# Where the query projection stands in a step of an fp32-exact attention kernel

## The reference

```
q, k, v = x Wq^T, x Wk^T, x Wv^T          # 32 query heads, 8 key/value heads, 128 wide
q, k = rope(rmsnorm(q)), rope(rmsnorm(k))
keys, values = cache (512 rows, by block table) + the 128 new ones
probs = softmax(q keys^T * scale, cached keys beyond the length masked)
x = x + (probs values) Wo^T
h = x W^T + 2 * sum over the top 2 of 8 experts of gate * (x A_e^T) B_e^T
x = x + h
```

## Time and profile before

| | |
|---|---|
| time, median of 3 runs | 1186.98 us (1186.64 to 1187.24) |
| the profiled execution | 1185.75 us |
| its span, first to last instruction | 1183.9 us |
| granted TensorE clock, mean of the span | 0.994 |
| TensorE matmul busy | 1147.6 us, 97% |
| TensorE weight loads (beside the matmuls) | 1023.2 us, 86% |
| ScalarE busy | 934.6 us, 79% |
| VectorE busy | 923.4 us, 78% |
| GpSimd busy | 766.8 us, 65% |
| DMA | 98.11 MB, 83 GB/s |

### The profile page before, as it was taken

One profiled execution on the slowest core, in us unless ns is written; L12 is line 12 of the kernel. 1 busy time (PEld: TensorE's weight loads), 2 busy tenths in 40 slices (PEclk: granted clock), 3 DMA queues, 4 the chain that ended last, 5 costly groups with the idle time before them and its releaser, 6 DMA issues.

```text
span 1183.9 us, 20774 instructions
## 1 busy us (share of the span) xinstructions
PE 1147.6 (97%) x6912; PEld 1023.2 (86%) x6912; DVE 923.4 (78%) x1880; ACT 934.6 (79%) x1830; POOL 766.8 (65%) x838
## 2 busy tenths in 40 slices
PE   3799999999999999999999999999999999999898
PEld 2688898998899888989988988889889889988787
DVE  6788888787778777887877787778878777877746
ACT  3788888888888888888888888888888888888741
POOL 5566676677676667676766766677667667666500
PEclk9899999999999999999999999999999999999999
DMA  6323412221222222122212222221222122121001
GB/s 239 124 82 97 147 50 91 95 89 53 94 95 66 76 94 94 50 92 94 86 56 94 94 64 78 94 94 50 92 94 83 57 92 92 61 64 55 19 1 72
DMA packets 53626, 98.11 MB, mean 83 GB/s; under 512 B 8592, under 2 KB 25872, under 8 KB 53264
## 3 DMA queue, kind: packets, MB, share of 16 engines
q1 hardware_dynamic: 41232, 63.21, 15.3%
q0 software_dynamic: 12288, 33.57, 9.6%
HBM read 90.45 MB, written 6.29 MB: 82 GB/s over the span
## 4 chain that ended last, share of the span: by engine, by line
PE 85%; DVE 5%; ACT 4%; issue 3%; DMA 1%; SPq 1%; POOL 0%; DVEq 0%; POOLq 0%
PE ps_s L1011 17%; PE ps_w L280 17%; PE ps_w L282 17%; PE ps_w L281 17%; PE ps_w L1042 9%; PE ps_w L1128 2%; PE ps_w L1110 2%; PE ps_s L993 2%; PE ps_w L1019 2%; ACT ps L527 2%; DVE pt_lo L664 2%; DVE ps L727 1%; ACT ps L533 1%; DMA y<-wo 1%; PE ps_w L1032 1%
## 5 line engine op out<-in xcount | busy, mean ns | idle before, releaser
L406 POOL DMA_INDIRECT kv_raw<-kv,rows x256 | 253.5, 990 | 93.9 <-issue 62.8
L527 ACT ACTIVATE ps<-ps,negmax 128x640 f32<-128x640 f32 x256 | 211.9, 828 | 95.1 <-DVE negmax L727 95.1
L664 DVE TENSOR_TENSOR pt_lo<-ps_w,pt_hi 128x512 fp32r<-128x512 f32 x322 | 209.9, 683 | 75.5 <-ACT pt_hi L538 74.3
L533 ACT ACTIVATE ps<-ps,recip 128x640 f32<-128x640 f32 x256 | 212.9, 832 | 67.5 <-DVE recip L734 67.5
L727 DVE CUSTOM_DVE_ANT_0 ps<-ps_s,mask 128x640 f32<-128x640 f32 x256 | 203.9, 815 | 1.2 <-PE ps_s L1011 1.1
L280 PE MATMUL ps_w<-w_hi,xt_hi 128*128 128x512 f32 (+1 forms) x512 | 188.7, 368 | 11.3 <-DVE w_lo L664 8.5
L282 PE MATMUL ps_w<-w_hi,xt_lo 128*128 128x512 f32 (+1 forms) x512 | 173.1, 338 | 0.0
L427 POOL TENSOR_TENSOR rot<-u,cos 128x640 f32<-128x640 f32 x64 | 101.7, 1589 | 109.9 <-DVE u L783 109.9
L281 PE MATMUL ps_w<-w_lo,xt_hi 128*128 128x512 f32 (+1 forms) x512 | 172.8, 337 | 0.0
L538 ACT ACTIVATE pt_hi<-ps_w 128x512 fp32r<-128x512 f32 x256 | 152.0, 594 | 19.4 <-PE ps_w L1042 14.6
L1042 PE MATMUL ps_w<-cst,ps 128*128 128x128 f32 x1024 | 154.0, 273 | 6.4 <-DVE pt_lo L664 5.9
(11 more groups left out here) (155 smaller groups left out, 2624.6 us busy)
## 6 DMA issues: line engine op xcount, KB each, us to landing
xt_hi<-xsplit SPq DMA_DIRECT2D x56, 256.0 KB, 3.4
xt_lo<-xsplit SPq DMA_DIRECT2D x56, 256.0 KB, 3.8
w_raw<-wqkv SPq DMA_DIRECT2D x56, 192.0 KB, 3.9
wo_raw<-wo SPq DMA_DIRECT2D x56, 128.0 KB, 4.2
kv_raw<-kv,rows POOLq DMA_INDIRECT x256
xsplit<-xt_hi SPq DMA_DIRECT2D x8, 256.0 KB, 2.4
xsplit<-xt_lo SPq DMA_DIRECT2D x8, 256.0 KB, 4.4
y<-x SPq DMA_DIRECT2D x2, 1024.0 KB, 6.6
```

The lines of the kernel that those rows point to most:

```text
L406: pool.indirect_dma_start(kv_raw[:, g % 2, t, :], None, kv[:, :], bass.IndirectOffsetOnAxis(rows[:, g % B, t:t + 1], 0)).then_inc(s_kv[g % ...
L527: nc.scalar.activation(ps[:, h, :], ps[:, h, :], ACT.Exp, bias=negmax[:, s % 2, h:h + 1], scale=-1.0, accum_out=rowsum[:, s % 2, h:h + 1]) ...
L533: nc.scalar.activation(ps[:, h, :], ps[:, h, :], ACT.Copy, scale=recip[:, s % 2, h:h + 1]).then_inc(a_norm, 1)
L664: return nc.vector.tensor_tensor(out_ap, full, hi.bitcast(F32), ALU.subtract)
```

## The change

In TensorE's step, Q (and `turn_x(s, "Q")`) moves from behind T0 to behind s1, and O moves from behind s1 to behind s2. The new order is s0, s1, Q, s2, O, T0, s3, T1, Y, and then as before. ScalarE takes the query copy behind `norm(1)`, then `exps(2)` and `norm(2)`, and only then `o_hi`, `probs(0)` and `v_hi`. VectorE takes `o_lo` behind `m2` instead of ahead of `rowmax(2)`. The ring of banks begins with Q, then O. GpSimd and the DMA queue of SyncE keep their order. No instruction is added or removed.

```diff
-UNITS = ["O", "T0", "Q", "T1", "Y", "T2", "QT", "KTC", "KV", "KTN", "T3", "TN"]
+UNITS = ["Q", "O", "T0", "T1", "Y", "T2", "QT", "KTC", "KV", "KTN", "T3", "TN"]
...
# ScalarE
                     norm(1)
                 if s == G:
                     expert_products(0)
-                if has(s - 1):
-                    wait(act, pe_o, s - 1)
-                    wait(act, pe_y, s - 2)
-                    nc.scalar.activation(o_hi[:], bank("O"), ACT.Copy).then_inc(a_o, 1)
...
-                if has(s):
-                    probs(0)
...
-                    exps(2)
-                    norm(2)
                 if has(g2):
                     wait(act, pe_q, g2)
                     wait(act, d_u, g2 - 2)
...
                     nc.scalar.activation(raw[:, g2 % 2, 0:QW], bank("Q"), ACT.Copy).then_inc(a_q, 1)
                 turn_x(s, "Q")
+                if has(s):
+                    exps(2)
+                    norm(2)
+                if has(s - 1):
+                    wait(act, pe_o, s - 1)
+                    wait(act, pe_y, s - 2)
+                    nc.scalar.activation(o_hi[:], bank("O"), ACT.Copy).then_inc(a_o, 1)
...
+                if has(s):
+                    probs(0)
...
# VectorE
-                if has(s - 1):
-                    wait(dve, a_o, s - 1)
-                    low(o_lo[:], bank("O"), o_hi[:]).then_inc(d_olo, 1)
...
                 if has(s):
                     rowmax(2)
...
                 if s == -1:
                     masks(B - 2, B)
                     biases()
+                if has(s - 1):
+                    wait(dve, a_o, s - 1)
+                    low(o_lo[:], bank("O"), o_hi[:]).then_inc(d_olo, 1)
...
                 if has(s):
                     rowmax(3)
                     probs(0)
# TensorE
                 if s == G:
                     second_layer(0)
+                if has(g2):
...
+                    three_passes(bank("Q"), [(xt_tile(xt_hi, g2, k), xt_tile(xt_lo, g2, k), wh[:, k, 0:QW], wl[:, k, 0:QW])
+                                             for k in range(KC)], before=weights_split).then_inc(pe_q, 1)
+                turn_x(s, "Q")
+                if has(s):
+                    scores(2)
                 if has(s - 1):
 
                     wait(pe, d_pt, s - 1, 5)
...
                 if has(s):
-                    scores(2)
                     turn_probs(0)
-                if has(g2):
...
-                turn_x(s, "Q")
                 if has(s):
                     scores(3)
                     turn_probs(1)
```

More of the change, by code:

```diff
@@ L564, in step @@
                     expert_products(0)
+                if has(g2):
+                    wait(act, pe_q, g2)
+                    wait(act, d_u, g2 - 2)
+                    if g2 == 1:
+                        act.wait_ge(d_mask, B)
+                    nc.scalar.activation(raw[:, g2 % 2, 0:QW], bank("Q"), ACT.Copy).then_inc(a_q, 1)
+                turn_x(s, "Q")
+                if has(s):
+                    exps(2)
+                    norm(2)
                 if has(s - 1):
@@ L794, in step @@
                     biases()
+                if has(s - 1):
+                    wait(dve, a_o, s - 1)
+                    low(o_lo[:], bank("O"), o_hi[:]).then_inc(d_olo, 1)
+                if s == G:
+                    for c in (1, 2):
+                        biased(c)
+                        add_base(c)
                 if has(s):
@@ L1049, in step @@
                     second_layer(0)
-                if has(s - 1):
[L1052 to L1061, removed]
-                if has(s):
-                    scores(2)
-                    turn_probs(0)
                 if has(g2):
@@ L1081, in step @@
                 turn_x(s, "Q")
+                if has(s):
+                    scores(2)
+                if has(s - 1):
+                    wait(pe, d_pt, s - 1, 5)
+                    wait(pe, p_v, s - 1, 2)
+                    wait_bank(pe, s, "O")
+                    three_passes(bank("O"), [(v_hi[:, t, :], v_lo[:, t, :],
+                                              pt_hi[:, t, :, :].rearrange("p h q -> p (h q)"),
+                                              pt_lo[:, t, :, :].rearrange("p h q -> p (h q)")) for t in range(KT)]
+                                 ).then_inc(pe_o, 1)
+                if s == G:
+                    second_layer(1)
+                    second_layer(2)
+                if has(s):
+                    turn_probs(0)
                 if has(s):
```

## The result

The kernel after takes 1193.86 us, median of 4 runs (1192.94 to 1194.86), beside 1186.9 us (1186.64 to 1187.24) for the kernel before: a ratio of 1.0062 with a 95% interval of 1.0051 to 1.0074. The forecast was 1191.5 us in a range of 1185 to 1200, slower with a chance of 0.70. The profiled execution took 1194.86 us with a span of 1193.1, against 1185.75 and 1183.9 before.

A forecast was written before the change was run, and what follows sets the result against it. TensorE, busy without a break in 56 middle steps, was taken as the bound. Profiled execution 1185.75 - 2.5 (middle) + 3.3 (early) + 3.6 (last two) + 0.3 (GpSimd) = 1190.4; median 1.2 above, given as 1191.5 us, range 1185 to 1200.

The forecast's parts named there:

- GpSimd's pause: GpSimd's occasional long pause, which hit nobody before, can now delay Y: +0.3 us.
- TensorE's own stream: Middle steps: O comes after its wait is past, so TensorE's pace alone is 17.07 us, not 17.13.
- The chain to Y: Middle steps: `o_lo` starts at 9.74, Y at 10.54 against 10.53 of TensorE's pace, so no slack is left.
- The port: Middle steps: `m2` starts 0.05 us ahead of `rot`, gets the port VectorE shares with GpSimd, and takes 0.82 us.
- The rival's total: GpSimd gets the shared port first in the middle steps: period 17.82 us, +39 us, about 1231; chance 0.11.
- Steps 0 to 5: Early steps: +0.3 us in step 0, +1.0 each in 1, 3 and 5, 0 in 2 and 4; together +3.3.
- The sign named for it: In steps 1, 3 and 5, Y waits about 2 us for `o_lo`.
- the small term: Step 0 has no O, but `rowmax(2)` comes later behind Q: +0.3 us.
- The start: Steps before the first scores: the prediction put nothing there, a term of 0.
- The step that failed: Q needs the bank that O had before, with the same wait; its ScalarE copy fits behind `norm(1)`.
- Steps 62 and 63: Last two steps: Y waits for VectorE to read the transposed result in its bank: +1.1 and +2.5, together +3.6 us.

The follow-up runs named there:

- d1: Kernel after plus a TensorE wait ahead of Q for the previous step's last low part of transposed probabilities, on a third chip: 1201.2 us.
- d3: Kernel after plus a 128x1 memset on VectorE behind `u` and its recip, with `m2` waiting for its semaphore: 1237.33 us.
- c1: Kernel after with nothing changed, on another chip: 1194.92 us, ratio 1.0069 to the kernel before.
- d4: Kernel after with nothing changed, the measure on a third chip: 1192.98 us, ratio 1.0055 to the kernel before.
- a2: Kernel after with the key positions staged in a corner of `ps` instead of `raw[:, 1]`: 1234.08 us.
- d2: Kernel after with key positions staged in `ps` and `w_lo` of the turned block ahead of `o_lo`: 1184.37 us, ratio 0.9985 to the kernel before.
- a1: Kernel after with VectorE's `w_lo` of the turned block moved ahead of `o_lo`, touching steps 61 to 63 alone: 1227.98 us.
- f1: Kernel after with key positions in `ps`, the turned block's `w_lo` ahead of `o_lo`, and weight splits behind the fourth reciprocal: 1211.51 us.
- f2: Kernel after with key positions in `ps` and the turned block's `w_lo` ahead of `o_lo`, run again on another chip: 1184.96 us.
- b4: Kernel before with VectorE's splits of the next head's weights moved behind the fourth reciprocal: 1275.11 us, ratio 1.0751.
- a3: Kernel after plus a 128x1 memset on VectorE between recip and `m2`, without a wait for it: 1234.53 us.
- a4: Kernel after plus a TensorE wait ahead of Q for the previous step's last low part of transposed probabilities, first chip: 1236.24 us.

## Why the forecast came out as it did

The medians differ by 7.0 us, forecast 4.5: the direction was right and the time lies in the range. The account below goes by the ledger of the profiled executions. Each term of the sum beside what it shows:

| term | forecast | measured |
|---|---|---|
| start, up to the first scores | 0 | +2.9 |
| step 0 | +0.3 | +0.9 |
| steps 1 to 5 | +3.0 | +2.9 |
| 56 middle steps, GpSimd's pause with them | -2.2 | -4.3 |
| step 62 | +1.1 | +2.7 |
| step 63 | +2.5 | +4.0 |
| sum | +4.7 | +9.1 |

**TensorE's own stream: right, a little small.** The step fell by 0.08 us, not 0.04 (and 0.04 times 56 is 2.2, not the 2.5 of the sum). The working said 17.07 for TensorE alone and 17.02 to 17.10 for the loop by the chain, and then took 17.09 "with some jitter". There was next to no jitter: 53 of the 56 middle steps take 17.05 or 17.06. d1 shows that the wait ahead of O is enough to explain the gain.

**The chain to Y: right.** `o_lo` starts at 9.75 of the step (9.74), Y at 10.57 (10.53). (The slack before is misread, 4.1 us: O ends at 5.33 and Y starts at 10.63, 5.3 by the measure that gives 1.67 now. No term uses it.)

**The port: right, and with its price.** `m2` won in all 56 middle steps of the kernel after with the 0.04 against 0.08 us seen in one step before, and d3 prices the other outcome at 17.81 a step (17.82). The rival's total, "about 1231", leaves out most of its own terms for the ends: with them it is 1233, and d3 took 1237.33. Nothing in the prediction says that a lead of 0.04 us seen once would hold 56 times, and the chance of 0.11 was a guess. It held in all middle steps of both other executions of this program (c1, d4); with the key positions moved it was lost in one step (below).

**Steps 0 to 5: right.** +0.94, +0.05, +0.93, +0.08 and +0.88 against +1.0, 0, +1.0, 0, +1.0. The sign named for it was about 2 us of wait at Y; it is 1.41 in step 1. In step 0 the small term was +0.9 and not +0.3: T2 waits 1.66 us for ScalarE there and QT 2.43 us for `rot` (0.41 and 2.64 in that step before), and products at half clock follow. Of this term the clock is the larger part: in d4, with the same waits, step 0 takes 16.37 us, less than the 16.60 before.

**The start: missed.** The step that failed is the one that treats the new ring of banks only for Q ("Q itself needs the bank that O had before, with the same wait") and for Y of the last steps. A ring in which every unit's place is its number modulo four also changes the neighbours of the units that run alone in steps -2 and -1. There Q and KV became each other's wait, and Q's copy is the one instruction that stands behind the masks. The runs show +2.9 us up to the first scores in its place. a2 and d2 bear it out: with the key positions elsewhere the first scores come 4 us sooner.

**Steps 62 and 63: right in mechanism, too small.** Y waits for `w_lo` as forecast. The places were worked out well: Y of step 62 starts 12.40 us behind its s0 (12.35), Y of step 63 3.7 later than before (3.7). The term that was left out is the clock: TensorE can run the products behind such a wait at half clock, 0.43 us apart. Where it doesn't, the two terms come out as forecast: step 62 in d4 is +1.1 (1.1), with KTN at 17.26 of the step (17.2), and step 63 in a2 is +2.4 (2.5). Where it does, each is 1.6 us longer: +2.7 and +4.0. The same wait is followed by either clock, and the runs don't tell what decides; behind the waits of 1.1 to 1.5 us of a1, d2, f1 and f2 the half clock came in none of eight. With the read moved ahead the two steps are shorter than before the change (33.2 us against 33.7).

The errors had both signs: 6.6 us of cost not forecast (3.5 at the start with step 0, 3.1 at the end) against 2.2 us of gain (2.1 in the middle, 0.1 in steps 1 to 5). That the sum is off by 4.4 us and not by 6.6 or more is luck.

## What to carry to other kernels

When an order of units sets which buffer each gets, write out the new pairs for the steps in which only some of the units run, at both ends: the steady state hides them. A wait on TensorE such as the two of 3.2 and 3.5 us here can cost more than its length, by the slow clock behind it (1.6 us each, in most executions), so what is moved in front of it should be the one short read that it waits for; and two executions of one kernel can differ by that much, so terms of 1 us at such places are compared over more than one trace. Where a step hangs on which of two engines takes a shared port first, count the order as part of the design: 0.12 us of delay on VectorE lost it in every step (+44 us here). Before a long operation is moved, look at what the other engine does at the new place (b4: a split of 0.54 us took 1.58 there, +89 us). And a time that fits a theory shows nothing until the instruction named by it has changed its length.

## What the runs showed of the hardware

- On one of the chips VectorE was held in nearly every middle step of four kernels: its second rowmax started 0.78 to 0.92 us behind the end of GpSimd's last indirect gather, with no release in the profile, at some 40 us in all. One of these files, run on another chip, was free of it (1236.24 and 1201.2 us). The kernel before took 1186.1 us on the first chip; its second rowmax starts 1.06 us before the gather's end, so it may be out of reach, or a delay may be hidden there: no trace of it was taken on that chip. In each of the four traces two steps, 27 and 55, had their gathers some 2 us later than usual, behind the rowmax; there was no hold in them, and they took 17.05 to 17.27 us, not 17.8. SyncE's transfers are issued at the same place of the step as in the kernel after, but these four traces have no landing for most of them, so a slower memory path on that chip can't be read or excluded. The hold is tied to the gathers in time; by what means GpSimd's gather would hold VectorE on one chip and not on others is open, and so is what the kernel after itself takes there.
- The clock behind one and the same wait differs between executions of one program: 3.53 us of idle ahead of Y in step 62 was followed by products 0.43 us apart in the kernel after and c1, and 3.52 us by products 0.23 apart in d4.
- a2, d2 and f2 lost the race for the port once each, in step 30, on three chips. In d2:

```profile
564.38 0.15 DVE L734 RECIPROCAL recip<-rowsum 128x1 f32<-128x1 f32 x1
564.66 2.14 DVE L784 TENSOR_TENSOR m<-u,sin 128x640 f32<-128x640 f32 x1
```

  `m2` starts 0.28 us behind the start of recip where it is 0.12 in the other steps, for no reason that the profile gives, and that step takes 17.78 us: 0.73 for 0.16 us. All three have the key positions moved, and no trace of the kernel after, of a1, a3, a4 or d1, without that edit, loses a middle step so. Being at the same place on three chips, it belongs to the program and not to chance. Their sibling f1, in which the splits are moved too, doesn't show it.
- A memset of 128x1 between recip and `m2` delayed `m2` by 0.01 us at most (a3); with a wait for its semaphore behind it, it delayed it by 0.12 us (d3).
